# Windowed attention of layer 2: subtracting the row maxima and summing the rows on VectorE, one exponential per bank of heads on ScalarE, and a new order of the work

## The reference, cut to what matters

```
qkv = (x @ Wqkv).reshape(B, T, 3, H, HD).transpose(2, 0, 3, 1, 4)
q, k, v = (qkv[0], qkv[1], qkv[2])
q = rope(q); k = rope(k)
attn = jnp.einsum('bhqd,bhkd->bhqk', q, k) * scale
mask = (j <= i) & (j > i - WIN)
attn = jnp.where(mask[None, None], attn, -jnp.inf)
attn = jax.nn.softmax(attn, axis=-1)
out = jnp.einsum('bhqk,bhkd->bhqd', attn, v)
out = out.transpose(0, 2, 1, 3).reshape(B, T, H * HD)
return out @ Wout
```

## Time and profile before

| what | value |
|---|---|
| median of 3 runs | 1496.78 us (1489.78 to 1500.4) |
| the profiled execution's own time | 1495.27 us |
| its span, first to last instruction | 1493.5 us |
| TensorE busy, share of the span | 77% |
| VectorE busy | 62% |
| ScalarE busy | 48% |
| GpSimd busy | 39% |
| granted TensorE clock, mean | 0.881 |

### The profile page before, as it was taken

The page is one execution under the profiler, slowest core; times in us unless marked ns, Lnnn a source line. Parts: engine busy times, 40 slices in busy tenths (PEclk is TensorE's granted clock), DMA queues, the critical chain, the costliest instruction groups (busy, mean ns, idle before and its releaser), DMA issues.

```text
span 1493.5 us, 13005 instructions
## 1 busy us (share of the span) xinstructions
...
## 2 busy tenths in 40 slices
...
DVE  4975788677877778455757788665653624423321
...
DMA packets 11270, 17.76 MB, mean 12 GB/s; under 512 B 1304, under 2 KB 7584, under 8 KB 10688
## 3 DMA queue, kind: packets, MB, share of 16 engines
...
## 4 chain that ended last, share of the span: by engine, by line
PE 36%; DVE 9%; ACT 5%; issue 2%; POOL 1%; POOLq 0%; DVEq 0%; ACTq 0%
PE bankE L1749 8%; PE bankE L1827 5%; PE bankE L1247 3%; PE bankS L1791 2%; PE bankS L1776 2%; PE bankE L1309 2%; PE bankE L1268 1%; ACT b_pr L1145 1%; PE bankS L1729 1%; DVE c_tw L1919 1%; PE bankE L622 1%; PE bankE L1297 1%; PE bankE L581 1%; PE bankE L1296 1%; DVE b_xr L1424 1%
## 5 line engine op out<-in xcount | busy, mean ns | idle before, releaser
L752 DVE TENSOR_TENSOR_SCAN hs<-dA,carry,bankS 128x512 f32<-128x512 f32 x128 | 156.7, 1266 | 3.3 <-DVE bankS L744 0.5
L1722 ACT ACTIVATE c_h<-bankE,C 128x512 f32<-128x512 f32 x144 | 99.0, 687 | 124.3 <-PE bankE L1827 123.9
L1749 PE MATMUL bankE<-c_h,c_w 128*128 128x512 f32 x288 | 150.7, 605 | 8.9 <-DVE c_tw L1919 6.8
L330 POOL TENSOR_TENSOR hc<-hs,cb 128x1024 f32<-128x1024 f32 x56 | 131.7, 2352 | 53.3 <-DVE hs L752 50.2
L307 POOL TENSOR_TENSOR cv<-cv,hc 128x1024 f32<-128x1024 f32 x56 | 132.5, 2366 | 4.4
L1618 POOL TENSOR_TENSOR c_acc<-c_acc,c_tw 128x512 f32<-128x512 f32 x32 | 40.8, 1274 | 198.0 <-DVE c_tw L1919 197.9
L1919 DVE SCALAR_TENSOR_TENSOR c_tw<-bankE,C,wb_ready 128x512 f32<-128x512 f32 x32 | 24.0, 751 | 128.0 <-PE bankE L1749 128.0
L1827 PE MATMUL bankE<-c_fH,c_w1H 128*128 128x512 f32 x144 | 101.1, 702 | 0.0
L445 ACT ACTIVATE sg<-bankE,C 128x512 f32<-128x512 f32 x80 | 54.5, 686 | 88.4 <-PE bankE L581 88.1
L744 DVE TENSOR_TENSOR bankS<-dx,bankS 128x1024 f32<-128x1024 f32 x64 | 78.4, 1225 | 8.4 <-PE bankS L510 7.7
L395 ACT ACTIVATE dA<-dl,Aneg 128x512 f32<-128x512 f32 x128 | 80.8, 709 | 3.3 <-DVE dl L735 3.2
...
## 6 DMA issues: line engine op xcount, KB each, us to landing
...
```

What stands on the lines that cost most here:

```text
L330: pool.tensor_tensor(dst[:, :, :], hs[:, k % HS, :, :], cb[:, k % 2, :].unsqueeze(1).to_broadcast([P, HV, G]), ALU.mult).then_inc(s["hc_re ...
L752: V.tensor_tensor_scan(hs[:, k % HS, h, :], dA[:, (HV * k + q) % DA, :], dbx[:, h, :], carry[:, k, h:h + 1], ALU.mult, ALU.add).then_inc(s ...
L1722: act.activation(h[:, n % 3, :], E[k % 2][:, :], ACT.Gelu_apprx_tanh, bias=col("b1_3", k)).then_inc(s["fs_ready"], 1)
L1749: pe.matmul(E[2][:, :], w2[:, k, :], h[:, n % 3, :], start=(f == 0), stop=(f == FB3 - 1)).then_inc(s["fdown"], 1)
```

## The change

Before, ScalarE made eight exponentials per step, one per head, each with the head's own bias (the negated scaled maximum) and each adding up its row. After, VectorE subtracts the maxima from the scores inside the PSUM bank, ScalarE makes one exponential per bank (three, three and two heads) with no bias and no sum, and VectorE adds up the rows of `pr` before it takes the reciprocals. The scaled negated maximum `nm` is gone. The heads are placed differently in the banks, and the banks are complete after the sixth, seventh and eighth product, where it was the fourth, seventh and eighth. C of the next step waits for 3 exponentials instead of 8.

More of the change, by code:

```diff
@@ L96 @@
 ORDER = [(p[0], p[1:].split(".")[0], int(p.split(".")[1])) for p in """
[L97 to L104, removed]
@@ new lines @@
+    an15.0 ao15.0 aB1.0 aB3.0 aB4.0 aB2.0 aF1.1 aR1.0 aF5.1 aM0.0 aF6.1 aF2.1 aR3.0 aF0.1 aF7.1 aR4.0 aM1.0 aF3.1 aF8.1 aF4.1 aF9.1 aN0.1
+    aM2.0 aM3.0 aA0.1 an0.1 ao0.1 aA1.1 aN1.1 an1.1 aM4.0 ao1.1 aN2.1 an2.1 aM5.0 aM6.0 aA2.1 ao2.1 aN3.1 an3.1 aM7.0 ao3.1 aN4.1 aM8.0
+    an4.1 aA3.1 aM9.0 ao4.1 aM10.0 aN5.1 an5.1 aM11.0 ao5.1 aN6.1 aM12.0 an6.1 aM13.0 ao6.1 aN7.1 an7.1 aM14.0 aM15.0 ao7.1 aA4.1 aN8.1
+    aL1.0 aL3.0 an8.1 aL4.0 ao8.1 aA5.1 aN9.1 aA6.1 aL5.0 aA7.1 an9.1 ao9.1 aN10.1 aR2.0 aU0.0 aU1.0 aU2.0 an10.1 ao10.1 aR5.0 aN11.1 aU3.0
@@ new lines @@
+    aN0.3 aR3.2 an0.3 ao0.3 aA2.3 aN1.3 an1.3 aM0.2 aR4.2 aM1.2 ao1.3 aN2.3 an2.3 aM2.2 ao2.3 aN3.3 aM3.2 aA3.3 an3.3 aM4.2 aM5.2 ao3.3
+    aN4.3 aM6.2 an4.3 aM7.2 ao4.3 aN5.3 aM8.2 an5.3 aM9.2 ao5.3 aN6.3 aM10.2 an6.3 aM11.2 aM12.2 aM13.2 ao6.3 aN7.3 an7.3 aM14.2 aM15.2
+    aL1.2 ao7.3 aL3.2 aA4.3 aA5.3 aA6.3 aN8.3 aL4.2 an8.3 ao8.3 aL5.2 aN9.3 aA7.3 an9.3 ao9.3 aR2.2 aU0.2 aN10.3 aU1.2 aR5.2 an10.3 aU2.2
+    aR6.2 aU3.2 ao10.3 aN11.3 aU4.2 aU5.2 an11.3 aU6.2 ao11.3 aN12.3 aU7.2 an12.3 aU8.2 ao12.3 aN13.3 aU9.2 an13.3 aU10.2 ao13.3 aN14.3
@@ new lines @@
+    bA11.0 bQ1.1 bA12.0 bQ2.1 bA3.0 bQ3.1 bK2.3 bX0.0 bX1.0 bX2.0 bK3.3 bX3.0 bX4.0 bX5.0 bK13.3 bX6.0 bX7.0 bA4.0 bA2.0 bC0.1 bA13.0 bc0.1
+    bA0.2 bN0.1 bC1.1 bV0.1 bH0.1 bK4.3 bc1.1 bN1.1 bK14.3 bW0.1 bO0.1 bC2.1 bK5.3 bV1.1 bH1.1 bc2.1 bK8.3 bW1.1 bO1.1 bN2.1 bC3.1 bV2.1
+    bH2.1 bc3.1 bW2.1 bN3.1 bO2.1 bV3.1 bH3.1 bW3.1 bA10.2 bO3.1 bK15.3 bK16.3 bK7.3 bA1.1 bQ0.2 bK9.3 bA11.1 bQ1.2 bA12.1 bK6.3 bQ2.2
+    bK10.3 bA3.1 bQ3.2 bX0.1 bX1.1 bX2.1 bX3.1 bX4.1 bX5.1 bX6.1 bX7.1 bK17.3 cI0.0 bA4.1 bA2.1 bC0.2 bc0.2 bA13.1 bN0.2 bA0.3 bC1.2 bV0.2
```

74 lines of the change are left out of this document (35 added, 39 removed).

## The result

| kernel | median | ratio to before, 95% interval |
|---|---|---|
| before | 1496.8 us (1489.8 to 1500.4) | |
| after | 1536.8 us (1535.3 to 1538.1) | 1.029 (1.024 to 1.033) |

What follows compares the result with a forecast made beforehand. It took VectorE as fullest in the first two attention stretches and TensorE as full from 1036 us on. Terms 7.1 - 3 + 2 + 0.8 gave +7 us, so 1503 us, range 1483 to 1516.

Steps and rivals of the forecast that it cites:

- Exponentials, maxima, subtractions, row sums as single instructions: Per step: exponentials 1.3 us instead of 3.1, maxima and subtractions 3.5 us, row sums 1.65 us without stretching.
- Sum on VectorE, "it fits, but not where it falls": VectorE over 16 steps: +3.3 us a step, +52 us in all, against 93.6 us of idle time.
- Latency, "the same": Scores to reciprocals in a step, VectorE otherwise free: about 5.3 us before and after.
- Group 0, +7.1: First attention group: later reciprocals in step 1 and V1's copies behind step 2's exponentials end it 7.1 us later.
- Given back before group 1, -3: Stretch between groups 0 and 1: K11.3's norm made earlier and fewer pieces beside it give back 3 us.
- Group 1, +2: Second attention group: +2.3 at V0, +3.3 in step 1, part given back by earlier starts and shorter exponentials; net +2 us.
- Group 2 +0.8, group 3 nothing: Last two attention groups: only step 0 of group 2 costs, 0.8 us; group 3, with TensorE full, costs nothing.
- 1.3 us of slack: Group 2, step 2: V2 starts 1.3 us later than reciprocals and GpSimd's work require, so the step costs nothing.
- Rest of the table, 0 within 5: Stages a and c: instructions only change places; taken as 0, with 5 us on either side.
- Sum: Whole kernel: 7.1 - 3 + 2 + 0.8 = +7 us, giving 1503 us.
- VectorE becomes the bound: Rival, groups 0 to 2: layer 1's pieces no longer hide under exponentials, +17 to +26 us; chance 0.20.
- Swallowed and paid: Rival: idle time swallows the new work and earlier starts and shorter exponentials pay, about -9 us, 1487; chance 0.22.

Runs made afterwards that it cites:

- e14: Kernel before plus three reductions of a constant on VectorE right behind each step's reciprocals, read by nobody: 1495.1 us.
- e15: Kernel before plus three reductions of a constant on VectorE ahead of each step's reciprocals, behind the wait for exponentials: 1522.4 us.
- e3: Changed kernel with the exponentials of steps 1, 2 and 3 of group 0 back at their places of before: 1529.0 us.
- e9: Changed kernel with 10 to 38 transposes of a constant in TensorE's waits behind C0 and C1 of groups 0 to 2 and V0 of group 0: 1528.9 us.
- e4: Changed kernel with the order of before for everything ahead of the attention of layer 2: 1532.9 us.
- e1: Changed code on the order of before, every place in the table as it was: 1526.1 us.

## Why the prediction was wrong, point by point

- *Exponentials, maxima, subtractions, row sums as single instructions*: right to 0.02 us for the reductions, 0.05 for the rest (0.67 against 0.65, 0.50 against 0.45). A step's maxima and subtractions take 3.5 us, its sums 1.60. No sum stretched: 643 ns in the median and 656 at most. The Trainium skill (SBUF — State Buffer, "Who interferes with whom") says that on trn2 a `tensor_reduce` never contends with GpSimd. This trace agrees, as far as it can: only 4 of the 32 sums of 480 columns ran wholly beside work of GpSimd, in 643 to 646 ns. ScalarE lost 22.9 us of busy time (713.4 us before), and more than 28 was said; the three more table loads came, 3.8 us.
- *Sum on VectorE, "it fits, but not where it falls"*: this step failed first. It measured the risk by occupied time, and e14 shows that 26 us of occupied time behind the reciprocals are free. The same work between scores and reciprocals cost 27 us (e15).
- *Latency, "the same"*: right only in the four steps in which nothing stands between (5.0 to 5.2 us). In most others, pieces of layers 1 to 3 that ran under the exponentials for nothing are now added to the chain: 11.3 us in step 1 of group 0, with K4 in it, 8.0 before. I had charged this in groups 0 and 1 (+2.9, +2.3, +3.3) and let it go in group 2.
- *The cuts.* The terms by group were cut at the ends of O and at the first maxima of a group, not at its reciprocals. Read to those cuts, these rows decide. The first fence is the changed kernel from V3.0 to the first maxima of group 1, the second the wait of TensorE in the same stretch before:

```profile
885.03 0.66 PE L1282 MATMUL bankS<-ident,b_pr 128*128 128x128 f32 x4 [1.52 <-POOL b_pr L1054]
...
893.68 2.07 PE L1304 MATMUL bankS<-b_wo,b_oaT 128*128 128x128 f32 x8 [0.69 <-ACT b_oaT L1158]
...
907.84 2.08 PE L1249 MATMUL bankE<-fT_ready,b_wsw 128*128 128x512 f32 x2 [3.42 <-DVE b_ra L1518]
...
941.24 0.65 DVE L1525 TENSOR_REDUCE b_m<-bankE 128x3 f32<-128x480 f32 x1
```

```profile
885.15 1.12 PE L1174 MATMUL bankS<-ident,b_xnS 128*128 128x128 f32 x4 [3.37 <-DVE b_xnS L1353]
```

- *Group 0, +7.1*: behind the end of layer 0 it measured +13.8, as O3 ended at 895.8 us and not at 877.2, and 4.7 of that came with layer 0. Of it 1.0 stands ahead of the first `ri`, 9.9 in g0 and 2.9 behind it. I followed the exponentials of step 2 ahead of V1's copies and overlooked those of step 1 ahead of V0's; e3, which moved both, gives back 7.8 us. And from V3 to the end of O3 I took 7.3 us from before, where it took 10.7, at the lower clock (eight products in 2.07 us against 1.16). With the waits filled (e9) it took 7.3.
- *Given back before group 1, -3*: measured +1.0, from the end of O3 to the first maxima of group 1 (45.4 us, 44.4 before). VectorE's shorter chain did not shorten it. TensorE waits 3.4 us there for rotary products, and it waited as long for K11.3's norm before: one wait took the place of the other.
- *Group 1, +2*: measured +6.6. 3.0 of it is step 0, 8.1 us from maxima to reciprocals where it was 5.1 (I had +2.3 for A13.0 and A0.2), and 3.6 is g1. The stretch from there to the maxima of group 2 is as before (+0.2).
- *Group 2 +0.8, group 3 nothing*: +1.8 in step 0 of group 2, +4.6 in g2 and +4.8 behind it, and -0.2 in group 3. Group 3, where TensorE is full, is as said. In g2 the reading of 1.3 us of slack held at full clock (27.1 us in e9, 27.6 before); what failed is that I had no term for the clock. Behind group 2 I had no term at all.
- *Rest of the table, 0 within 5*: +4.7 at the end of layer 0, where e4, with the old order there, ends at its old place and is 3.9 us faster in all. Within the bound, and with a sign: five profiles with the new order end layer 0 at 801 to 809 us, fifteen with the old one at 797 to 803.
- *Sum*: 4.7 + 13.8 + 1.0 + 6.6 + 0.2 + 1.8 + 4.6 + 4.8 - 0.2 + 2.7 (R) = 40.0 us, where I had 7.
- *The rivals*: "VectorE becomes the bound" had the right sign and named the pieces that no longer hide, at 17 to 26 us; the code alone costs 30 (e1). But its name is wrong: VectorE is not a bound, and the 1.3 us of stretch from which it was to decide never came. So its nearness to the time is partly luck. "Swallowed and paid" did not happen. Its sum was also unclear: half of 18.5 us is 9.2, and the 5 that it uses is only the share that shorter exponentials save of it.

What stays open: how the 30 us of the code split between the time from scores to reciprocals, the pieces ahead of the next maxima and the clock, and what the new places of the heads cost. The filled kernels gave back 2 to 8 us; executions at an equal clock put the clock's part of the 30 at 5 to 17, as an estimate.
